# Ternary weights by rounding into one-byte subnormals, with the sign taken at the eviction

## The reference, cut to what matters

```python
def _quant_weight(w):
    s = jnp.clip(jnp.mean(jnp.abs(w)), EPS, None)
    wq = jnp.clip(jnp.round(w / s), -1.0, 1.0) * s
    return w + jax.lax.stop_gradient(wq - w)
# w1: (4096, 1024), w2: (1024, 4096), both float32
h = jax.nn.gelu(_bitlinear(x, w1), approximate=False)
return _bitlinear(h, w2)
```

## Time and profile before

| | us |
|---|---|
| time before, median of 3 runs (1055.4 to 1057.2) | 1056.78 |
| span of the profiled execution, first to last instruction | 1054.4 |
| median less span (launch and end) | 2.4 |
| PE busy | 979.3 (93%) |
| DVE busy | 737.9 (70%) |
| ACT busy | 467.1 (44%) |
| POOL busy | 128.0 (12%) |

### The profile page before, as it was taken

The page is one execution under the profiler, slowest core; times in us unless marked ns, Lnnn a source line. Parts: engine busy times, 40 slices in busy tenths (PEclk is TensorE's granted clock), DMA queues, the critical chain, the costliest instruction groups (busy, mean ns, idle before and its releaser), DMA issues.

```text
span 1054.4 us, 17446 instructions
## 1 busy us (share of the span) xinstructions
PE 979.3 (93%) x6781; PEld 533.9 (51%) x6781; DVE 737.9 (70%) x1038; ACT 467.1 (44%) x573; POOL 128.0 (12%) x139
## 2 busy tenths in 40 slices
PE   1799899996899999999969999899999999999998
PEld 0688655553555666665534444444444444444444
DVE  7999888877664555668679754999977555555541
ACT  5344446553355565566522113999733122222221
POOL 6300042320311111000043100011000000000000
PEclk9899899998899999999989999999999999999999
DMA  3800026665778898885446855788513554444441
GB/s 121 243 2 2 2 81 227 244 228 193 233 293 306 324 350 323 318 320 204 159 162 182 215 128 178 278 319 310 186 40 71 120 120 113 109 109 109 110 98 36
DMA packets 166145, 188.91 MB, mean 179 GB/s; under 512 B 126520, under 2 KB 126842, under 8 KB 161984
## 3 DMA queue, kind: packets, MB, share of 16 engines
q1 hardware_dynamic: 159679, 165.47, 49.1%
q0 software_dynamic: 6400, 22.55, 6.5%
HBM read 137.98 MB, written 35.33 MB: 164 GB/s over the span
## 4 chain that ended last, share of the span: by engine, by line
PE 74%; DVE 14%; issue 6%; DMA 3%; ACT 2%; POOL 0%; DVEq 0%; SPq 0%; ACTq 0%; POOLq 0%
PE ps L1095 20%; PE ps L1293 13%; PE ps L1322 12%; PE ps L1202 8%; PE ps L1218 6%; DVE fq L2276 3%; PE ps L1275 2%; PE ps L1159 2%; DMA eo_d<-eo 2%; DVE w1l L2111 2%; PE ps L982 1%; PE ps L955 1%; DVE stats L1775 1%; PE ps L973 1%; DVE o_key L1854 1%
## 5 line engine op out<-in xcount | busy, mean ns | idle before, releaser
L1293 PE MATMUL ps<-w1q,xqt 128*128 128x512 fp8e4 x640 | 139.9, 379 | 0.4 <-issue 0.4
L1656 ACT ACTIVATE hf<-ps,fs 128x512 f32<-128x512 f32 x80 | 54.9, 688 | 183.2 <-PE ps L1293 183.2
L1322 PE MATMUL ps<-w2q,hqt 128*128 128x512 fp8e4 x576 | 126.4, 379 | 0.0
L2360 DVE TENSOR_REDUCE hm<-hf 128x1 f32<-128x512 f32 x80 | 54.2, 685 | 73.8 <-ACT hf L1656 73.8
L1293 PEld LDWEIGHTS ps<-w1q,xqt 128*128 128x128 f16 x640 | 62.4, 98 | 75.8 <-issue 0.9
L1322 PEld LDWEIGHTS ps<-w2q,hqt 128*128 128x128 f16 x576 | 56.3, 98 | 66.9
L1095 PE MATMUL ps<-wt_h,xt 128*128 128x512 f16 x320 | 85.4, 379 | 0.0
L1095 PE MATMUL ps<-gwt_h,xt 128*128 128x512 f16 x320 | 84.5, 379 | 0.6 <-issue 0.6
L1202 PE MATMUL ps<-xdh,w1h 128*128 128x314 f16 x256 | 77.1, 301 | 6.2 <-ACT ht L1566 3.3
L1202 PE MATMUL ps<-xdh,w1l 128*128 128x314 f16 x256 | 76.4, 299 | 0.0
L1202 PE MATMUL ps<-xdl,w1h 128*128 128x314 f16 x256 | 76.3, 298 | 0.0
(11 more groups left out here) (320 smaller groups left out, 1949.5 us busy)
## 6 DMA issues: line engine op xcount, KB each, us to landing
wstage<-in_L_ffn_w SPq DMA_DIRECT2D x32, 1024.0 KB, 10.9
abs_in<-in_L_ffn_w SPq DMA_DIRECT2D x18, 1024.0 KB, 6.5
abs_e<-in_L_ffn_w SPq DMA_DIRECT2D x14, 1024.0 KB, 5.1
fnat_b<-in_L_ffn_w SPq DMA_DIRECT2D x28, 512.0 KB, 6.4
fnat_a<-in_L_ffn_w SPq DMA_DIRECT2D x27, 512.0 KB, 4.8
eo_d<-eo SPq DMA_DIRECT2D x16, 512.0 KB, 3.1
hq_d<-hq SPq DMA_DIRECT2D x8, 1024.0 KB, 6.3
xs_d<-xs_all SPq DMA_DIRECT2D x10, 512.0 KB, 2.9
```

The costliest lines, as they stand in the source:

```text
L1293: last = mm(ps[:, n % 4, :], xqt[:, u, k, :], w1q[:, k // 2, n * 512:(n + 1) * 512, k % 2], start=(k == 0), stop=(k == KD - 1))
L1322: last = mm(ps[:, 4 + h, :], hqt[:, u, k, :], w2q[:, k // 2, h * 512:(h + 1) * 512, k % 2], start=(k == 0), stop=(k == KF - 1))
L1656: cp(hf[:, i % 2, n * 512:(n + 1) * 512], ps[:, n % 4, :], ACT.Gelu, scale=fs[:, i % 2, 3:4]).then_inc(s_ge, 1)
L2360: last = v.tensor_reduce(hm[:, u, n:n + 1], hf[:, u, n * 512:(n + 1) * 512], AX.X, ALU.max, apply_absolute_value=True)
```

## The change

ACT's sign ahead of the conversion is gone, with its tile `fsgn` and its semaphore. DVE multiplies the weights with 2^-9/s and writes one-byte floats; 2^-9 is the smallest step of that format, so the conversion rounds to whole multiples of it. `fq` has four buffers in place of two. DVE now waits for the load itself, and for the turn of piece n - 4. PE turns the bytes as before. ACT evicts them with the function Sign, byte by byte (1024 elements of a partition) in place of a copy of 512 pairs. Since ACT now handles single bytes, the even and odd rows of `w1` are sorted by the load: partition p = 64a + z of a piece takes row 2z + a.

```diff
+TINY = 2.0 ** -9
...
-            f1v = f1_in.rearrange("(n p) d -> n p d", p=P)
+            f1v = f1_in.rearrange("(n z a) d -> n a z d", a=2, z=P // 2)
             f2v = f2_in.rearrange("(n p) (b d) -> b n p d", p=P, b=4)
...
-                packed = fq[:, n % 2, :].bitcast(F16)
+                packed = fq[:, n % 4, :].bitcast(F16)
...
-                if i >= NT - 2:
-                    act.wait_ge(s_swh, 1)
-                    for n in range(2 * (i - NT + 2), 2 * (i - NT + 2) + 2):
-                        upper_sign(n)
...
-            def upper_sign(n):
-
-                act.wait_ge(s_fn[n % NF], 16 * (n // NF) + 16)
-                if n >= 4:
-                    act.wait_ge(s_fq, 4 + n - 3)
-                cp(fsgn[:, n % 4, :], fnat[n % NF], ACT.Sign, bias=sw[:, 4 + n // 32:5 + n // 32],
-                   saturate=False).then_inc(s_fsgn, 1)
...
-                if 4 <= n + 3 < 64:
-                    upper_sign(n + 3)
...
-                    part = w1p[:, :, 256 * (n // 2):256 * (n // 2) + 256].rearrange("p c (a z) -> p c a z", a=2)
-                    cp(part[:, :, :, 64 * (n % 2):64 * (n % 2) + 64], blocks.rearrange("p (c z a) -> p c a z", c=KD // 2, a=2),
-                       ACT.Copy).then_inc(s_fc, 1)
+                    part = w1p[:, :, 512 * (n // 2):512 * (n // 2) + 512].rearrange("p c (a z) -> p c a z", a=2)
+                    cp(part[:, :, :, P * (n % 2):P * (n % 2) + P], blocks.rearrange("p (c a z) -> p c a z", c=KD // 2, a=2),
+                       ACT.Sign, saturate=False).then_inc(s_fc, 1)
...
-                v.tensor_scalar(sw[:, 4:6], sw[:, 2:4], 0.5, None, ALU.mult).then_inc(s_swh, 1)
+                do(v.tensor_scalar(sw[:, 6:8], sw[:, 2:4], 1.0 / TINY, None, ALU.mult))
+                v.reciprocal(sw[:, 4:6], sw[:, 6:8]).then_inc(s_swh, 1)
                 dve.wait_ge(s_swh, 1)
-                do(v.tensor_scalar(sw[:, 6:8], sw[:, 2:4], -0.5, None, ALU.mult))
...
             def weight_piece(n):
 
                 m = n // 32
-                dve.wait_ge(s_fsgn, n + 1)
-                dve.wait_ge(s_ft, n + 1)
-                v.scalar_tensor_tensor(out=fq[:, n % 2, :], in0=fnat[n % NF], scalar=sw[:, 4 + m:5 + m],
-                                       in1=fsgn[:, n % 4, :], op0=ALU.is_gt, op1=ALU.min, saturate=False).then_inc(s_fq, 1)
+                dve.wait_ge(s_fn[n % NF], 16 * (n // NF) + 16)
+                if n >= 4:
+                    dve.wait_ge(s_ft, 2 + n - 3)
+                v.tensor_scalar(fq[:, n % 4, :], fnat[n % NF], sw[:, 4 + m:5 + m], None, ALU.mult,
+                                saturate=False).then_inc(s_fq, 1)
```

More of the change, by code:

```diff
@@ L307, in build_kernel @@
         restart("misc", misc_mark)
-        fq = sb("misc", "fq", [P, 2, D], F8)
-        fsgn = sb("misc", "fsgn", [P, 4, D], F8)
+        fq = sb("misc", "fq", [P, 4, D], F8)
         restart("misc", misc_mark)
@@ L446, in build_kernel @@
         s_hsfix = sem("s_hsfix")
-        s_fsgn = sem("s_fsgn")
-        s_fneg = sem("s_fneg")
         s_fq = sem("s_fq")
@@ L1610, in h_high @@
                 cp(flat[:, bass.ds(i * D, D)], h32[:, :], ACT.Copy, scale=dinv[:, 1, bass.ds(i, 1)]).then_inc(s_hsh, 1)
-            def upper_sign(n):
-                act.wait_ge(s_fn[n % NF], 16 * (n // NF) + 16)
-                if n >= 4:
-                    act.wait_ge(s_fq, 4 + n - 3)
-                cp(fsgn[:, n % 4, :], fnat[n % NF], ACT.Sign, bias=sw[:, 4 + n // 32:5 + n // 32],
-                   saturate=False).then_inc(s_fsgn, 1)
-            w1p = w1q[:, :, :, :].rearrange("p c f a -> p c (f a)").bitcast(I16)
-            w2p = w2q[:, :, :, :].rearrange("p c f a -> p c (f a)").bitcast(I16)
+            w1p = w1q[:, :, :, :].rearrange("p c f b -> p c (f b)")
+            w2p = w2q[:, :, :, :].rearrange("p c f b -> p c (f b)")
             spare = slice(LAST - 2, LAST - 2 + SEL)
@@ L1636, in _ @@
                 act.wait_ge(s_ft, 2 + n + 1)
-                blocks = bank16(4 + n % 4)[:, 0:D // 2].bitcast(I16)
+                blocks = bank16(4 + n % 4)[:, 0:D // 2].bitcast(F8)
                 if n < 32:
-                    part = w1p[:, :, 256 * (n // 2):256 * (n // 2) + 256].rearrange("p c (a z) -> p c a z", a=2)
-                    cp(part[:, :, :, 64 * (n % 2):64 * (n % 2) + 64], blocks.rearrange("p (c z a) -> p c a z", c=KD // 2, a=2),
-                       ACT.Copy).then_inc(s_fc, 1)
+                    part = w1p[:, :, 512 * (n // 2):512 * (n // 2) + 512].rearrange("p c (a z) -> p c a z", a=2)
+                    cp(part[:, :, :, P * (n % 2):P * (n % 2) + P], blocks.rearrange("p (c a z) -> p c a z", c=KD // 2, a=2),
+                       ACT.Sign, saturate=False).then_inc(s_fc, 1)
                 else:
                     b, o = (n - 32) // 8, (n - 32) % 8
-                    cp(w2p[:, 4 * b:4 * b + 4, o * P:(o + 1) * P], blocks.rearrange("p (c z) -> p c z", c=KD // 2),
-                       ACT.Copy).then_inc(s_fc, 1)
+                    cp(w2p[:, 4 * b:4 * b + 4, 2 * P * o:2 * P * (o + 1)], blocks.rearrange("p (c z) -> p c z", c=KD // 2),
+                       ACT.Sign, saturate=False).then_inc(s_fc, 1)
             def hidden_t(q, last):
```

## The result

The changed kernel takes 1302.14 us (median of 5 runs, 1301.06 to 1307.66) beside 1055.5 us (5 runs, 1054.56 to 1057.2): a ratio of 1.2349, with a 95% interval of [1.2329, 1.2368] (the ratios on record aren't exactly the quotients of the two medians). The forecast was 1307, with a range of 1287 to 1332. The profiled execution took 1303.26 us, its span is 1301.4; before, the span was 1054.4, so 247.0 us have come in.

What follows compares the result with a forecast made beforehand. DVE was taken to bound the aggregation tiles, but `w1` loads on two engines to decide: piece 31 comes 252.5 us later, 2.5 us is regained, net +250.0, span 1304.4, with 2.4 around it 1307 us (1287 to 1332).

Steps and rivals of the forecast that it cites:

- The bound and the gains: Aggregation stage: DVE bounds the tile; conversion falls to 0.75 us, eviction grows to 1.02, gaining some 10 us by these parts alone.
- Two engines: `w1` loads: a source with two outer steps goes to two DMA engines, 64 rows each, despite 128 partitions; chance 0.85.
- The same two engines, one load at a time: `w1` loads: always the same two engines, loads standing in line, 10.16 us each, 32 loads 325.1 us.
- The rival of changing pairs: `w1` loads: two engines each but other ones each time, seven loads side by side, 1056 us (1051 to 1062); chance 0.04.
- The sum: Whole kernel: piece 31 252.5 us later, 2.5 us gained behind it, net +250.0, span 1304.4 us.
- a load on two engines: `w1` loads: 524,288 bytes, half on each engine at 25.8 GB/s, 10.16 us a load.
- the share of `xt`: Last linear tile's transfer, queued among `w1` loads on the two engines: its part there put at 4 us.
- piece 31 turned: PE's transposes of the last `w1` piece: at 961.1 us, where it was 708.6 before.
- piece 31 to piece 63: `w2` half on PE: 45.2 us plus 1.5 for first loads and 3 for the clock, 49.7 against 52.2.
- The clock's 3 us: PE at the start of the `w2` half: 3 us added for running at clock 0.50 after idling.
- The last linear tile: Linear stage: `xt` arrives late behind `w1` loads, so this tile begins near 660 us in place of 638.
- The rival on the other side: `w1` loads: all 16 engines carry them, PE allows 10.21 us a tile, 1047 us (1043 to 1051); chance 0.08.

## Why the prediction was right, point by point

**The bound and the gains.** DVE was the bound, as read from the earlier trace rows: with plain loads the tile falls to PE's 10.20 us, and with a conversion of 1.28 us it is back at 11.56. Conversion 0.75 (said 0.75) and eviction 1.02 (said 1.02) were read off the nearest rows. The gain by these parts alone was put at some 10 us, with 1047 us (1043 to 1051) for plain loads over 16 engines; it is 12.6, and 1042.6 us: 1.36 us a tile, not 1.16. I had let the loads limit a tile at 10.4 us, with the rate of before, 352 GB/s. They went at 376 GB/s (share 0.99), faster than a tile of 10.2 us asks, so PE was the limit. Why they went faster than before is not shown.

**Two engines.** The step on which all hung, that 2 outer steps give two engines though the other end has 128 partitions, holds: two small packets for a load, and 4 for 4. The Trainium skill (DMA: Bandwidth & Descriptors, section "Why a DMA increments its semaphore by 16 and not by 1") has this rule, the largest number up to 16 that divides the slowest dimension of both ends; the counts of 2, 4, 8 and 16 now show it for unequal ends.

**The same two engines, one load at a time.** Held: steps of 9.98 us that don't overlap. The rival of changing pairs is out; it asked for a stage as fast as before.

**The sum** came out 3.0 us too high (span 1304.4, measured 1301.4). Its terms were mis-sized in opposite directions, so the closeness of the total is in part luck:

| term | said | measured |
|---|---|---|
| a load on two engines | 10.16 us (25.8 GB/s each) | 9.98 us (26.3 each); over 31 gaps -5.6 us |
| the share of `xt` | 4 us | 2.4 us (12.35 - 9.98) |
| the last two `w1` loads | nothing | +3.8 us (10.66 and 13.08, not 9.98) |
| piece 31 turned | 961.1 | 957.3 (956.73 + 0.61) |
| piece 31 to piece 63 | 49.7 us | 50.2 us (to 1007.55) |
| piece 63 to feed-forward | 9.9 us | 10.1 us (to 1017.68) |

The rate came from stretches in which 16 engines ran together; an engine in a pair is 2% faster. The term that I had not seen is the end of the `w1` loads. From 938 to 950 us the share is 0.6 to 1.0, so `w2` loads were running on the other engines while pieces 30 and 31 (landed at 942.8 and 955.9) were still on the way. The 3.8 us lost are three times the 1.27 us that a `w2` load takes on an engine, so I read it as `w2` rows on the same two engines; no row shows it directly. I had charged such a mixture (1.5 us) only to the time after piece 31. The turns of pieces 31 and 32, from PE's timeline, and piece 32's conversion from DVE's:

```profile
956.73 0.61 PE L1061 MATMUL ps<-id,fq 128*128 128x128 f16 x4 [10.76 <-DVE fq L2261]
957.13 1.06 PE L1273 MATMUL ps<-hs_h,at_h 128*128 128x512 f16 x2
...
960.58 0.61 PE L1061 MATMUL ps<-id,fq 128*128 128x128 f16 x4 [1.54 <-DVE fq L2261]
...
959.77 0.75 DVE L2261 TENSOR_SCALAR fq<-fnat_a,sw 128x1024 fp8e4<-128x1024 f32 x1
```

That the time from piece 31 to piece 63 came out near 49.7 us is luck in one term. PE did wait 1.54 us for piece 32, about the 1.5 us of the sum, but not for a load: DVE had `agg` and the statistics of a tile to do first and began the conversion without a gap behind them.

The clock's 3 us were about right. A pair of products takes 1.06 us here and 0.59 at the clock of 1.00: PE runs at the lower of its two levels (0.50, 1.2 of 2.4 GHz) after idling, as taken from the earlier trace rows, and is back at 1.00 in the window from 970 us. Pieces 32 to 35 took 5.8 us (960.58 to 966.38) where three blocks of 1.09 were counted, 2.5 us more. In the slow stretch PE worked 2.6 us in 10 (26.17 in 100), not 1.1 as said, since a tile's three blocks without a piece are done there too and the clock is near 0.5.

**The last linear tile** was said to begin near 660 us; its first product starts at 662.23, after 19.6 us of waiting for `xt`. It cost nothing in the end, since piece 31 was 295 us away.

**The rival on the other side** was priced nearly right for plain loads (1047, 1043 to 1051, for 1042.6 measured) and was wrong in its condition. I wrote that it decides from 14 engines on, at 1.45 us a load. Three kernels had all 16 engines busy and still took about 2.2 us a load (231 to 238 GB/s): how the rows are spread matters too, in the halves by the side of the partitions. My row for it, a plain 128-row load, has a good spread, and I took the engine count for the whole of it.

| kernel | us | ratio |
|---|---|---|
| the change | 1302.14 | 1.2349 |
| before, with the change's loads | 1310.62 | 1.2425 |
| the change, 4 outer steps | 1146.13 | 1.0864 |
| the change, 8 outer steps | 1087.01 | 1.0301 |
| the change, 16 outer steps | 1056.93 | 1.0003 |
| the change, two transfers a load | 1055.95 | 1.0001 |
| the change, plain loads sorted at the eviction | 1042.63 | 0.9871 |
| this, conversion of 1.28 us | 1053.21 | 0.9982 |
| this, loads in two halves | 1058.69 | 1.0016 |
| this, loads in three parts | 1051.54 | 0.9965 |

## What to carry to other kernels

A transfer that is reordered for free at its source isn't free: look at its outermost step at both ends first, since two steps put 512 KB on two engines (9.98 us), and check it in a trace by the small packets for each load and by GB/s beside the DMA share. A full share with 235 GB/s in place of 376 is a sign to look at how the rows are split, so keep one transfer over all 128 partitions, in their plain order, which was the fastest here. Sort where an engine has time to spare: here ACT's second eviction (0.17 us more a piece, off the path) kept the plain load and won 12.6 us.

## What the runs showed of the hardware that was not expected

- All 16 engines busy can mean 376 to 394 GB/s or 231 to 238, with the same rows of 4 KB and the same share of 1.0: with 64 partitions on one side at a time, or with a block of eight neighbouring partitions to each engine, an engine moves 14.4 to 14.9 GB/s; in a pair or in a group of four it moves 26.3.
- Eight engines went from 130 to 210 GB/s in the middle of one stage, with nothing changed in what they were given.
- SP itself is held up when its loads are slow. In the changed kernel's timeline of SP (start, us, transfer), beside the earlier trace rows:

```profile
626.78 9.39 SPq L693 DMA_DIRECT2D fnat_b<-in_L_ffn_w  x3
636.28 23.89 SPq L685 DMA_TRANSPOSE xt<-xt_d  x1
660.22 8.79 SPq L693 DMA_DIRECT2D fnat_a<-in_L_ffn_w  x3
```

Issuing three loads took 9.39 us in place of 2.92, and the transpose 23.89 in place of 3.93: with two or three loads in line the next issue takes about as long as a load does. So only a few of the seven buffers had a load under way at a time. That cost nothing here, as the two engines never ran empty (53 GB/s until about 938 us), but another transfer that SP had to issue would probably have come late by as much, as `xt` did.
